# Wavelet attention: maxima in one stream, six tiles ahead across groups of heads; the output stored in five pieces

## The reference, cut to what matters

```python
xe, xo = (x[:, 0::2], x[:, 1::2])
a = (xe + xo) * inv
det = (xe - xo) * inv
q = (a @ wq).reshape(B, L, nh, hd)      # L = 1024, nh = 16, hd = 8
k = (a @ wk).reshape(B, L, nh, hd)
v = (a @ wv).reshape(B, L, nh, hd)
att = jnp.einsum('bqhd,bkhd->bhqk', q, k) * (1.0 / np.sqrt(hd))
att = jax.nn.softmax(att, axis=-1)
o = jnp.einsum('bhqk,bkhd->bqhd', att, v).reshape(B, L, D) @ wo
```

## Time and profile before

| what | value |
|---|---|
| median of 3 runs | 4379.03 us (4377.32 to 4381.64) |
| the profiled execution's own time | 4358.43 us |
| its span, first to last instruction | 4357.1 us |
| PE, DVE, ACT, POOL busy | 83%, 76%, 65%, 23% of the span |
| phase C, from its first maximum to the last exponential's end | about 595 to 1098 us |

### The profile page before, as it was taken

One profiled execution on the slowest core, in us unless ns is written; L12 is line 12 of the kernel. 1 busy time (PEld: TensorE's weight loads), 2 busy tenths in 40 slices (PEclk: granted clock), 3 DMA queues, 4 the chain that ended last, 5 costly groups with the idle time before them and its releaser, 6 DMA issues.

```text
span 4357.1 us, 74462 instructions
## 1 busy us (share of the span) xinstructions
PE 3635.9 (83%) x28950; PEld 1917.7 (44%) x28950; DVE 3294.0 (76%) x5091; ACT 2845.8 (65%) x4856; POOL 1001.8 (23%) x1479
## 2 busy tenths in 40 slices
PE   6999868999799998999997666666666659899998
PEld 4666522222344445666665112222222215566776
DVE  6787767777311127887886999999999996778887
ACT  3655415556344445666664999999999995566665
POOL 2444432100467640000001232322332220000000
PEclk8999959999999999999998555555555559899999
DMA  1000032331511200000000111111110110000000
GB/s 48 1 1 1 1 69 38 54 58 20 114 26 37 39 17 9 12 7 12 2 2 16 22 22 22 22 22 22 22 19 19 22 20 21 7 12 7 7 2 21
DMA packets 256813, 97.51 MB, mean 22 GB/s; under 512 B 223795, under 2 KB 241854, under 8 KB 256446
## 3 DMA queue, kind: packets, MB, share of 16 engines
q1 hardware_dynamic: 256462, 92.74, 10.8%
HBM read 31.75 MB, written 2.23 MB: 8 GB/s over the span
## 4 chain that ended last, share of the span: by engine, by line
PE 41%; DVE 29%; issue 12%; ACT 6%; DMA 1%; POOL 0%; SPq 0%; DVEq 0%; ACTq 0%; POOLq 0%
DVE d_negmax L2825 14%; PE psum L2351 7%; PE psum L2380 6%; DVE f_m_E L2450 6%; PE psum L2366 6%; PE psum L2055 5%; PE psum L2077 5%; ACT d_junk L2883 3%; DVE wl_negmax L1563 3%; PE psum L1443 2%; PE psum L1432 2%; DVE f_pT_E L2469 2%; PE psum L1420 2%; ACT wl_p L1704 1%; DVE residual L2480 1%
## 5 line engine op out<-in xcount | busy, mean ns | idle before, releaser
L2825 DVE TENSOR_REDUCE d_negmax<-psum 128x1 f32<-128x1024 f32 x1024 | 1170.9, 1210 | 25.4 <-PE psum L2761 23.4
L2883 ACT ACTIVATE d_junk<-psum,d_negmax 128x1024 bf16<-128x1024 f32 x1024 | 1136.0, 1125 | 37.1 <-DVE d_negmax L2825 32.6
L2761 PE MATMUL psum<-d_qT,d_kT 64*128 64x512 bf16 x2048 | 622.9, 604 | 432.1 <-ACT d_junk L2883 414.9
L2544 ACT ACTIVATE hidden<-psum,f_nm_E 128x1024 f32<-128x1024 f32 x512 | 566.0, 1112 | 143.5 <-DVE f_nm_E L2453 143.4
L2450 DVE TENSOR_REDUCE f_m_E<-psum 128x1 f32<-128x1024 f32 x512 | 601.6, 1216 | 46.8 <-PE psum L2351 45.6
L2351 PE MATMUL psum<-f_k_E,f_q_swapped_E 64*128 64x512 f32 x1024 | 526.9, 624 | 6.6 <-ACT hidden L2544 6.6
L2351 PE MATMUL psum<-f_k_E,f_q_E 64*128 64x512 f32 x1024 | 526.6, 624 | 2.9 <-DVE f_v_E L2441 1.9
L2551 ACT COPY f_pT_E<-psum 128x512 f32<-128x512 f32 x512 | 299.4, 585 | 322.3 <-PE psum L2366 322.3
L2380 PE MATMUL psum<-f_pT_E,f_v_E 128*64 128x128 f32 x8192 | 505.0, 276 | 2.5 <-DVE residual L2480 2.5
L2761 PEld LDWEIGHTS psum<-d_qT,d_kT 64*128 64x128 bf16 x2048 | 107.9, 101 | 842.9 <-ACT d_junk L2883 761.1
L2469 DVE COPY f_pT_E<-psum 128x512 f32<-128x512 f32 x512 | 351.3, 686 | 159.5 <-PE psum L2366 150.0
(11 more groups left out here) (331 smaller groups left out, 4736.3 us busy)
## 6 DMA issues: line engine op xcount, KB each, us to landing
moe_gates_on_all<-moe_gate_spill SPq DMA_DIRECT2D x16, 1024.0 KB, 11.9
f_q_swapped_E<-f_q_E SPq DMA_DIRECT2D x64, 128.0 KB, 2.3
moe_w<-in_moe_w SPq DMA_DIRECT2D x15, 256.0 KB, 6.5
out<-residual SPq DMA_DIRECT2D x1, 2048.0 KB, 8.7
residual<-in_hidden_states SPq DMA_DIRECT2D x2, 768.0 KB, 7.3
wl_qT<-wl_q_rows SPq DMA_TRANSPOSE x48, 3.3
residual<-in_hidden_states SPq DMA_DIRECT2D x2, 256.0 KB, 3.5
m_taps<-in_m_conv SPq DMA_DIRECT2D x4, 128.0 KB
```

Of the source, the lines that this page charges most:

```text
L2544: A.activation(pb[:, u % 2, f * 2 * BANK:(f + 1) * 2 * BANK], two(2 * f), ACT.Exp, bias=nm[:, u % 4:u % 4 + 1], scale=SC, accum_out=rs[:, ...
L2761: last = T.matmul(bank(2 + 2 * (at % 3) + jj), kT[half, s, jb * P:(jb + 1) * P], qT[half, s, hf * BANK:(hf + 1) * BANK], start=True, stop= ...
L2825: V.tensor_reduce(mh[:, t % 2, n // 2, n % 2:n % 2 + 1], two(2 + 2 * (at % 3)), X, ALU.max, negate=True).then_inc(*maxed.up(at))
L2883: A.activation(junk[:, at % 3, :], two(2 + 2 * (at % 3)), ACT.Exp, bias=mh[:, t % 2, n // 2, n % 2:n % 2 + 1], accum_out=sh[:, t % 2, n // ...
```

## The change

Phase C. All maxima of all rounds become one list `ahead`; each round's shift hangs behind its last maximum. Before round 0, the first 38 of them are put in (32 plus LEAD = 6), then exactly one at each unit, until the list is empty. So a round's shift falls at unit 25 of the round before, units 26 to 31 carry the first six maxima of the round after next, and from unit 26 of round 6 on there are none. The value products of a round's last quad move to units 2 and 3 of the next round (`pe_av_behind`); the copy out of PSUM is cut in two halves, one at each of those units, with a signal for each; `norm` moves from unit 5 to unit 6. The last phase's SP stores the result in five pieces (blocks 0 to 15, 16 to 23, 24 to 27, 28 to 30, 31), each as soon as its last block is summed, and `finish` only waits.

```diff
+        store = loads("store")
+        out_rows = out.rearrange("b (i p) d -> p (b i) d", p=P)
+        stored = [(0, NT), (NT, NT + NT // 2), (NT + NT // 2, R - 4), (R - 4, R - 1), (R - 1, R)]
...
-                seq += maxes(0, 0) + [("shift", 0, 0)]
+                LEAD = 6
+                ahead = []
+                for n, r in enumerate(rounds_c):
+                    ahead += [[m] for m in maxes(*r)]
+                    ahead[-1].append(("shift", *r))
+                for _ in range(4 * CT + LEAD):
+                    seq += ahead.pop(0)
...
-                    if n:
-                        seq.append(("fin", *rounds_c[n - 1]))
-                    ahead = []
-                    if n + 1 < len(rounds_c):
-                        ahead = maxes(*rounds_c[n + 1])
                     for u in range(4 * CT):
                         seq.append(("exp", b, g, u // 4, u % 4))
-                        for _ in range(1 + (u % 7 == 3)):
-                            if ahead:
-                                seq.append(ahead.pop(0))
-                                if not ahead:
-                                    seq.append(("shift", *rounds_c[n + 1]))
+                        if ahead:
+                            seq += ahead.pop(0)
+                        if n and u in (2, 3):
+                            seq.append(("fin", *rounds_c[n - 1], u - 2))
...
-                        if u == 5 and n:
+                        if u == 6 and n:
                             seq.append(("norm", *rounds_c[n - 1]))
...
-                    if kt and hh in (2, 3):
-                        pe_av(b, g, kt - 1, hh - 2)
+                    pe_av_behind(quad_at[b, g, kt], hh)
...
                     if j == 0:
                         T.wait_ge(*exped(b, g, kt, 3))
-                        if kt == 0 and round_at[b, g]:
-                            T.wait_ge(*oc_done(*rounds_c[round_at[b, g] - 1]))
+                    if kt == 0 and round_at[b, g]:
+                        T.wait_ge(*oc_done(*rounds_c[round_at[b, g] - 1], j))
...
+                def pe_av_behind(q, hh):
+
+                    if q and hh >= 2:
+                        pe_av(q - 1, hh - 2)
...
-                def dve_fin(b, g):
-                    V.wait_ge(*valued(b, g, CT - 1, 1))
-                    if round_at[b, g]:
+                def dve_fin(b, g, j):
+                    V.wait_ge(*valued(b, g, CT - 1, j))
+                    if round_at[b, g] and j == 0:
                         V.wait_ge(*o_turned(*rounds_c[round_at[b, g] - 1], 1))
-                    V.tensor_copy(oc[:, :], two(6)).then_inc(*oc_done.up(b, g))
+                    V.tensor_copy(oc[:, j * BANK:(j + 1) * BANK], bank(6 + j)).then_inc(*oc_done.up(b, g, j))
...
                     sp_swap(3)
+                    if tag == "E2":
+                        for lo, hi in stored:
+                            b, i = (hi - 1) // NT, (hi - 1) % NT
+                            SP.wait_ge(*summed(((b * NPAIR + NPAIR - 1) * NT + i), 1))
+                            SP.dma_start(out_rows[:, lo:hi, :], res[:, lo:hi, :]).then_inc(*store.one())
...
-            enter(SP)
-            store = loads("store")
-            SP.dma_start(out.rearrange("b (i p) d -> p (b i) d", p=P), res[:, :, :]).then_inc(*store.one())
             SP.wait_ge(*store.all())
```

More of the change, by code:

```diff
@@ L1267, in phase_C @@
                             seq.append(("spread", *rounds_c[n + 2]))
-                seq += [("fin", *rounds_c[-1]), ("norm", *rounds_c[-1])]
+                seq += [("fin", *rounds_c[-1], 0), ("fin", *rounds_c[-1], 1), ("norm", *rounds_c[-1])]
                 seq += [("co", 1), ("wo", 1)] + [("conv", 1, c) for c in range(4)] + [("yt", 1, 0), ("yt", 1, 1)]
@@ L1310, in phase_C @@
                 quads = [(b, g, kt) for b, g in rounds_c for kt in range(CT)]
+                quad_at = {q: n for n, q in enumerate(quads)}
                 valued = signal("valued", [(*q, j) for q in quads for j in range(2)])
-                oc_done = signal("out_copied", rounds_c)
+                oc_done = signal("out_copied", [(*r, j) for r in rounds_c for j in range(2)])
                 o_turned = signal("out_turned", pair("norm", 2))
@@ L1433, in pe_exp, with pe_av @@
                     last.then_inc(*second_pass.up(b, g, kt, hh))
-                def pe_av(b, g, kt, j):
+                def pe_av(q, j):
+                    b, g, kt = quads[q]
                     if j == 0:
                         T.wait_ge(*exped(b, g, kt, 3))
-                        if kt == 0 and round_at[b, g]:
-                            T.wait_ge(*oc_done(*rounds_c[round_at[b, g] - 1]))
+                    if kt == 0 and round_at[b, g]:
+                        T.wait_ge(*oc_done(*rounds_c[round_at[b, g] - 1], j))
                     for hh in range(4):
@@ L1446, in pe_av @@
                     last.then_inc(*valued.up(b, g, kt, j))
+                def pe_av_behind(q, hh):
+                    if q and hh >= 2:
+                        pe_av(q - 1, hh - 2)
                 def pe_norm(b, g):
-                    T.wait_ge(*oc_done(b, g))
+                    T.wait_ge(*oc_done(b, g, 1))
                     bk = pe_slot("norm", b, g)
@@ L1489, in pe @@
                             pe_exp(*u)
-                        elif kind == "fin":
-                            for half in range(2):
-                                pe_av(*u, CT - 1, half)
+                        elif kind == "fin" and u[:2] == list(rounds_c[-1]):
+                            pe_av(len(quads) - 1, u[2])
                         elif kind == "norm":
```

## The result

The changed kernel took 4332.66 us (median of 5 runs, 4323.26 to 4337.45), the kernel before 4377.32 us (median of 5, 4363.70 to 4381.64) in the same comparison. The ratio is 0.990, with an interval of 0.9878 to 0.9921: 44 us less, between 35 and 53. The profiled execution took 4323.26 us, its span is 4321.9 us, against 4357.1: 35.2 us less.

The account below looks back on a forecast made before the run. No engine full; in phase C, PE and DVE each pace two units of four. Gains 16.8 + 2.5 + 1.9 − 1.3 + 6.1 + 2.0 + 6.5 = 34.5 us off 4379.0 gave 4344.5 us, range 4328 to 4367.

Parts of the forecast that it names:

- A plain round: Phase C, rounds 1 to 6: 51.5 us a round against 54.27, 2.8 us less each, 16.8 us in all.
- The end of the stream and its start: Phase C: 1.9 us less where maxima run out from round 6's unit 26; 1.3 us more before the first second tile.
- Round 0: Phase C's first round, with layer-norm pieces on DVE: 2.5 us less.
- The change from round 1 to 2: Phase C: PE's wait for transposed rows and the slow clock behind it mostly go, 6.1 us less.
- The clock elsewhere: Phase C: shorter gaps may remove clock dips in round 5 and uncosted rounds, 2.0 us less, between 0 and 4.
- The store: End of the kernel: five DMAs for one leave 64 KB behind the last sum, landing in 2.2 us: 6.5 us less.
- I take the difference over unchanged: Whole kernel: the runs' median stays 20.6 us above the profiled execution, 4379.03 against 4358.43 us.
- Only the store pays: Rival, phase C: mean stretch of four units 6.6 us, 20 us of gain lost, 4364 us; chance 0.15.
- Slower: Rival, phase C: DVE becomes the bound, all stretches of four units go at 7.10 us, 4398 us; chance 0.03.

Follow-up runs that it names:

- experiments 8 and 9: Changed kernel with the value products' halves in units 1 and 3 (8), there also behind the second tile, ahead of the maximum (9): 4350.02 us, 4363.68 us.
- experiment 6: Changed kernel with three maxima ahead over the change of round (LEAD = 3), so the shift falls at unit 28: 4353.27 us.
- experiment 3: Changed kernel with no maxima ahead over the change of round (LEAD = 0), so the shift falls at unit 31: 4407.92 us.
- experiment 5: Changed kernel with the old placing of maxima; the lag of the value products, half copies and five stores stay: 4386.23 us.
- experiment 4: Changed kernel with the last quad's value products and their copies back in front of the next round's first unit, six maxima ahead kept: 4333.12 us.
- experiment 11: Changed kernel with value products in quarters of 256 columns, one behind the maximum of every unit: 4381.71 us.
- experiment 12: Changed kernel with quarters of the value products behind each maximum in rounds 3 to 6 only, halves elsewhere: 4323.77 us.

## Why the prediction was right, and where its terms were off

- **A plain round, 51.5 us.** Measured 51.20. Eight times 6.25 held over 32 units in a row. Norm 1.03 (forecast 1.1), half copies 0 (0), shift 0.11 (0.4). The 6.25 was a measured row, which is why it held; the prediction's reason for it, two units bound by PE and two by DVE, was refuted (experiments 8 and 9).
- **The end of the stream and its start.** Round 6 gave 5.6 us for 4.7. The start cost 1.30 us, forecast +1.3 by the rule that PE can begin when the slot three places before is read; the tile's row shows this wait for a maximum.
- **Round 0, 2.5 us.** It gave 4.3, of which 2.6 is its change to round 1 (3.56 us from the last exponential to the next before, 0.92 after). The clock was low in it for 13 us both times, so the term was mis-sized by itself.
- **The change from round 1 to 2, 6.1 us.** The two stretches of rows 7 now read as in any other change, so the whole 7.1 us (4.2 and 2.9) came; the 1 us taken off for POOL was too much. Rounds 1 and 2 gave 13.8 us, 8.2 more than two plain gains of 2.8; a fall of 3.4 us in round 1, at 704.6, is gone too. One DVE operation of the shift did meet POOL (1.13 us beside POOL's 1.04), and cost less than 1 us. The Trainium skill (GPSIMD Engine Reference, 8. Key points) speaks of DVE instructions in a 2-port mode or with two SBUF inputs; the one that met POOL here, and one more in experiment 6 at 1.10 us, was a cast with one input, of whose mode the trace says nothing. With the shift three units later (experiment 6) the rule's case came in full: 1.97 us beside 2.17.
- **The clock elsewhere, 2.0 us.** Rounds 3 and 5 gave 1.5 us each beyond their 2.8, round 4 0.6. Round 7 gave 1.7 back, by the lag and not by the clock; no term had that. Together 1.9, so the 2.0 came out by two errors that cancel. By rounds the whole effect of the clock can be estimated: rounds 1 to 5 gave 10.5 us beyond 3.07 each, of which 3.3 is the longer step over the change from 1 to 2; the other 7 or so go with 34 us less of low clock. The prediction had 2.9 and 2.0 for it.
- **The store, 6.5 us.** Measured 7.3 in its own stretch: 64 KB landed in 1.5 us, nearer to the row of 1.6 than to the 2.2 taken. The Trainium skill (DMA: Bandwidth & Descriptors, Rules for kernel authors) asks to coalesce many small transfers into one large one, and calls those under 64 KB mostly overhead; no piece here is smaller than that. For this last store the measurement decides against one large transfer, since all pieces but one land beside compute.
- **Sum.** Phase C: 28.0 forecast, 32.8 measured. Profiled execution: near 4324 forecast, 4323.3 measured. That it agrees so closely is luck: phase C and the store gave 5.6 us more than forecast, and the unchanged code took 4.9 us more.
- **The median.** The forecast was 12 us too high. Of this 1.7 is the kernel before, whose median in the comparison was 4377.32 and not 4379.03. The other 10 are "I take the difference over unchanged", the one step that was clearly off: the medians differ by 44.7 us, the profiled executions by 35.2. The base was high. Beside the experiments the kernel before ran 59 times more: median 4371.65, from 4360.0 to 4381.9. Each run lists its mean clock over the span: the four at 0.818 took 4378.5 to 4381.9 us, the four at 0.823 took 4360.0 to 4364.7, and the correlation over all is −0.92. The profiled execution, at 0.823, was of the second kind. Against 4371.65 the changed kernel's median is 39 us lower, 4.5 over the forecast. That the draw of the clock makes the difference is a correlation, not shown by an experiment.
- **The rivals.** "Only the store pays" needed quads of 6.6 us; none was. "Slower" by DVE was far: DVE was busy 4.81 of 6.25 us. But a slower outcome was near in another way, which the prediction didn't name: experiments 3 and 5 show that with the lead missing either half of the change is slower than before, by waits and by the clock behind them.

What each part is worth: the store 7.3 us (outside C); the lag about 5 us once the lead is there (experiment 4); the lead over the change 85 us of C against none (554.7 less 470.0). Of these the waits themselves, about 6.7 us at each of seven changes, are 47; the other 38 go with 123 us more of low clock. The even pace takes away what the doubled units cost, 0.47 + 0.86 + 0.85 = 2.2 us a round.

## What to carry to other kernels

Where a pass over one group feeds the next through a slow step (here six small DVE operations and four transposes), run the first pass as one stream over all groups with a fixed lead that just covers the step, at one item for each item of the second pass. Price each wait of PE twice: once as idle time, once as the stretch behind it at half clock; in experiment 3 the waits were 47 us and what went with the clock 38, and in experiment 5 the clock was the larger part. And read a small term from its own stretch of the trace, not from two spans.

## What was unexpected of the hardware

- PE kept busy at the lower clock level didn't always get the higher one back. With quarters of 256 columns it was busy 59.78 of 60 us at 0.50, and the clock stayed there until 735.3 us; with halves of 512 columns it rose at 653.6. In experiment 11 PE made nothing but maxima, second tiles and quarters from 640 to 733 us. At 733.09 came a group of fp32 transposes (128x128, L243, x8 in the trace), and the clock rose at 735.3. It fell again at 783.1; the next such group came at 811.88 (L1466), and it rose at 813.8. Two shorter falls in quartered rounds, at 957.2 there and at 907.8 in experiment 12, also ended within 4.0 us of the start of such a group. That these transposes brought the clock back is not shown; no experiment moved them.
- A full clock also fell with no wait ahead of it: at 1049.58 in the changed kernel and at 1090.3 in experiment 11, both times inside the router's matmuls of 8 columns, with PE busy in all of the 6.9 and 7.3 us before.
- Runs of one kernel spread over 22 us (0.5%), in step with the mean clock that they were granted.
- The time beside POOL of small DVE operations also grows for those with one SBUF input. The trace of before already has it, at the change of rows 6: two casts of the shift took 1.13 and 1.11 us there, which the prediction didn't read. DVE and POOL in the changed kernel at the same moment:

```profile
744.52 1.13 DVE L1580 CAST wl_q_rows<-wl_negmax_rest 128x32 bf16<-128x32 f32 x1
744.52 1.04 POOL L1554 CAST wl_parts<-wl_q 128x1024 bf16<-128x1024 f32 x1
```

The cast took as long as POOL's, 1.1 us; elsewhere it takes 0.25.
